# GpSimd normalises every row tile but the last, and four engines get new written-out orders

## The reference

```
mask = adj > 0                                  # adj is 4096 x 4096, about 0.4% of it set
head = mask / max(sqrt(sum(mask, axis=-1)), 1e-12)
inc  = adj + head
y    = x + (inc @ x) / sum(inc, axis=-1)        # x is 4096 x 256
out  = (y - mean(y)) / sqrt(var(y) + 1e-5)      # over the 256 columns of a row
```

## Time and profile before

| | us |
|---|---|
| median of 3 runs | 413.19 |
| lowest and highest run | 411.52, 413.34 |
| profiled execution | 410.89 |
| span of its trace | 409.1 |

### The profile page before, as it was taken

One profiled execution on the slowest core, in us unless ns is written; L12 is line 12 of the kernel. 1 busy time (PEld: TensorE's weight loads), 2 busy tenths in 40 slices (PEclk: granted clock), 3 DMA queues, 4 the chain that ended last, 5 costly groups with the idle time before them and its releaser, 6 DMA issues.

```text
span 409.1 us, 8775 instructions
## 1 busy us (share of the span) xinstructions
PE 389.3 (95%) x2224; PEld 343.1 (84%) x2224; DVE 364.2 (89%) x757; ACT 371.4 (91%) x507; POOL 346.3 (85%) x222
## 2 busy tenths in 40 slices
PE   1689999999999999999999999999999999999995
PEld 0668889988888878888888888888888888888884
DVE  0897999999999999999999999999999999999932
ACT  4967999999999999999999999999999999998530
POOL 3111599999999999999999999999999999999970
PEclk9999999999999999999999999999999999999999
DMA  8999997576677667667666665767666666670020
GB/s 237 269 253 253 264 261 215 168 238 204 200 221 222 190 187 215 190 206 222 200 208 205 195 205 191 208 216 214 197 210 201 196 206 192 215 218 27 27 64 13
DMA packets 36183, 80.00 MB, mean 196 GB/s; under 512 B 9536, under 2 KB 17728, under 8 KB 36160
## 3 DMA queue, kind: packets, MB, share of 16 engines
q1 hardware_dynamic: 35776, 78.68, 66.1%
q10 hardware_dynamic: 384, 1.05, 0.8%
HBM read 75.50 MB, written 4.19 MB: 195 GB/s over the span
## 4 chain that ended last, share of the span: by engine, by line
PE 83%; POOL 4%; issue 4%; SPq 4%; DMA 3%; DVE 1%; ACT 1%; POOLq 0%; ACTq 0%
PE edge L1307 46%; PE edge L1321 23%; PE edge L1258 12%; POOL inc_split L564 3%; DMA x_stage<-in_x_dram 3%; SPq L156 3%; PE sums L1253 1%; SPq L179 1%; DVE incT L767 1%; POOL inc_split L578 0%; PE sums L1232 0%; SPq L184 0%; POOL small L548 0%; DVE inc L751 0%; ACT scaled L251 0%
## 5 line engine op out<-in xcount | busy, mean ns | idle before, releaser
L564 POOL TENSOR_TENSOR inc_split<-incT,inc_split 128x960 fp32r<-128x960 f32 x120 | 269.4, 2272 | 2.4 <-ACT inc_split L262 0.5
L1307 PE MATMUL edge<-x_split,inc_split 128*128 128x512 f32 (+1 forms) x930 | 223.4, 392 | 0.1
L1307 PEld LDWEIGHTS edge<-x_split,inc_split 128*128 128x128 f32 x930 | 168.1, 188 | 32.8 <-ACT inc_split L262 0.9
L751 DVE SCALAR_TENSOR_TENSOR inc<-raw,scaled 128x1024 f32<-128x1024 f32 x128 | 154.3, 1206 | 3.3 <-ACT scaled L251 2.4
L767 DVE STREAM_TRANSPOSE incT<-inc 128x1024 f32<-128x1024 f32 x128 | 156.3, 1230 | 0.7 <-PE edge L1258 0.4
L251 ACT ACTIVATE scaled<-raw,small 128x1024 f32<-128x1024 f32 x128 | 141.1, 1107 | 2.8 <-DVE inc L751 1.2
L240 ACT ACTIVATE sign_out<-raw 128x1024 int8<-128x1024 f32 x128 | 133.7, 1045 | 4.5 <-DMA raw<-in_adj_dram 4.3
L1321 PEld LDWEIGHTS edge<-x_split,inc_split 128*128 128x128 f32 x900 | 112.2, 191 | 2.3
L1321 PE MATMUL edge<-x_split,inc_split 128*128 128x256 f32 x900 | 113.5, 283 | 0.0
L262 ACT CAST inc_split<-incT 128x960 fp32r<-128x960 f32 x90 | 86.5, 984 | 0.7 <-DVE incT L767 0.7
L583 POOL TENSOR_TENSOR small<-small 128x1 f32<-128x1 f32 x24 | 13.2, 554 | 37.2 <-DVE small L733 37.0
(11 more groups left out here) (42 smaller groups left out, 138.8 us busy)
## 6 DMA issues: line engine op xcount, KB each, us to landing
raw<-in_adj_dram SPq DMA_DIRECT2D x504, 128.0 KB, 2.5
rows<-in_x_dram SPq DMA_DIRECT2D x32, 128.0 KB, 2.1
out_dram<-rows SPq DMA_DIRECT2D x32, 128.0 KB, 1.7
x_stage<-in_x_dram SPq DMA_DIRECT2D x12, 256.0 KB, 9.4
raw<-in_adj_dram ACTq DMA_DIRECT2D x8, 128.0 KB, 5.1
x_stage<-in_x_dram SPq DMA_DIRECT2D x4, 192.0 KB, 13.6
x_native<-in_x_dram SPq DMA_DIRECT2D x4, 64.0 KB, 5.7
```

The source lines that it names most:

```text
L564: nc.gpsimd.tensor_tensor(lo_of(s, q), incT[:, s, 0:SPLIT, q, :], hi_of(s, q).bitcast(fp32), ALU.subtract).then_inc(lo_by_pool, 1)
L751: nc.vector.scalar_tensor_tensor(inc[:, q, :], raw[:, s, q, :], 0.0, scaled[q % 2][:, :], ALU.is_gt, ALU.add, accum_out=part_sums[:, s, 0, ...
L1307: last = nc.tensor.matmul(edge[s][:, c0:c1], inc_split[s][:, 0, b, :, :].rearrange("p q j -> p (q j)"), x_split[:, b, :, :].rearrange("p h ...
```

## The change

1. `shift_of`, the `shift` columns and its semaphore are gone. `normalise_by_dve` is gone from DVE, and `normalise` from ACT.
2. POOL gets a `normalise(t, s)` for tiles 0 to 30: one `tensor_scalar`, (y - mean) * rstd, both factors being columns of one element per partition. Tile 31 stays on DVE.
3. In the loop the wait for 1/std stands on the instruction before it (`low_quarter(..., rstd_of_tile=...)`).
4. The orders of ACT, DVE and POOL, and the places of the sums on PE, are new: the written-out part now covers tiles 0 to 17, and the loops start at tile 18. SP's list is not changed.

```diff
 # ACT
-            def normalise(t, s):
-                act.wait_ge(shift_ready, t - 3)
-                nc.scalar.activation(y[:, s, :], y[:, s, :], ACT.Identity, scale=norm_rstd[:, s, G:G + 1],
-                                     bias=shift[:, s:s + 1]).then_inc(result_ready, 1)
 # POOL
+            def normalise(t, s, alone=0, own=True):
+                if alone:
+                    pool.wait_ge(rstd_ready, alone)
+                elif own:
+                    pool.wait_ge(norm_ready, t + 5 - EARLY)
+                nc.gpsimd.tensor_scalar(y[:, s, :], y[:, s, :], mean_var[:, s, 0:1], norm_rstd[:, s, G:G + 1],
+                                        ALU.subtract, ALU.mult).then_inc(result_ready, 1)
-            with pool.Fori(7, PAIRS - 2) as u:
+            with pool.Fori(9, PAIRS - 2) as u:
                 norm_of(2 * u + 1, 1)
                 low_quarter(2 * u, 0, 0, behind=1)
                 round_quarter(2 * u, 0, 1, own=False)
-                low_quarter(2 * u, 0, 1)
+                low_quarter(2 * u, 0, 1, rstd_of_tile=2 * u - 3)
+                normalise(2 * u - 3, 1, own=False)
                 low_quarter(2 * u, 0, 2)
                 low_quarter(2 * u, 0, 3)
...
 # POOL, the end
             low_quarter(31, 1, 1)
+            normalise(28, 0, alone=3)
             low_quarter(31, 1, 2)
             low_quarter(31, 1, 3)
             rstd_of(30, 0)
+            normalise(29, 1, alone=4)
+            normalise(30, 0, alone=5)
             rstd_of(31, 1)
 # ACT's loop, one tile of the two
-                scale_quarter(2 * u, 0, 2)
                 sign_quarter(2 * u + 1, 1, u, 2)
                 sign_quarter(2 * u + 1, 1, u, 3)
+                scale_quarter(2 * u, 0, 2)
                 round_quarter(2 * u, 0, 0)
                 scale_quarter(2 * u, 0, 3)
                 sign_quarter(2 * u + 2, 0, u + 1, 0)
                 scale_quarter(2 * u + 1, 1, 0)
-                sign_quarter(2 * u + 2, 0, u + 1, 1)
                 scale_quarter(2 * u + 1, 1, 1)
-                normalise(2 * u - 3, 1)
                 round_quarter(2 * u, 0, 2)
                 round_quarter(2 * u, 0, 3)
-                scale_quarter(2 * u + 1, 1, 2)
+                sign_quarter(2 * u + 2, 0, u + 1, 1)
                 sign_quarter(2 * u + 2, 0, u + 1, 2)
                 sign_quarter(2 * u + 2, 0, u + 1, 3)
+                scale_quarter(2 * u + 1, 1, 2)
...
 # DVE's loop, one tile of the two, as it is after
+            with dve.Fori(9, PAIRS - 2) as u:
                 inc_quarter(2 * u, 0, 0)
+                inc_quarter(2 * u, 0, 1)
                 degree(2 * u - 2, 0)
+                transpose_quarter(2 * u, 0, 0)
+                transpose_quarter(2 * u, 0, 1)
+                inc_quarter(2 * u, 0, 2)
+                count_of(2 * u + 1, 1)
                 inverse_degree(2 * u - 2, 0)
                 y_first(2 * u - 2, 0, u - 1)
+                transpose_quarter(2 * u, 0, 2)
+                inc_quarter(2 * u, 0, 3)
                 y_second(2 * u - 2, 0)
+                transpose_quarter(2 * u, 0, 3)
                 statistics(2 * u - 2, 0)
                 mean_variance(2 * u - 2, 0)
                 variance_eps(2 * u - 2, 0)
-                shift_of(2 * u - 3, 1)
...
```

More of the change, by code:

```diff
@@ new lines, in _ @@
+            sign_quarter(18, 0, 9, 1)
+            round_quarter(16, 0, 3)
+            scale_quarter(17, 1, 2)
+            sign_quarter(18, 0, 9, 2)
+            sign_quarter(18, 0, 9, 3)
+            scale_quarter(17, 1, 3)
+            sign_quarter(19, 1, 9, 0)
+            round_quarter(17, 1, 0)
+            scale_quarter(18, 0, 0)
+            scale_quarter(18, 0, 1)
+            sign_quarter(19, 1, 9, 1)
+            round_quarter(17, 1, 2)
+            round_quarter(17, 1, 3)
+            with act.Fori(9, PAIRS - 2) as u:
@@ L638, in _ @@
             low_quarter(6, 0, 3)
+            norm_of(8, 0)
             round_quarter(7, 1, 1)
-            norm_of(8, 0)
+            normalise(4, 0)
             low_quarter(7, 1, 0)
@@ L647, in _ @@
             round_quarter(8, 0, 1)
+            normalise(5, 1)
             low_quarter(8, 0, 1)
@@ L652, in _ @@
             round_quarter(9, 1, 1)
+            normalise(6, 0)
             low_quarter(9, 1, 0)
@@ L656, in _ @@
             low_quarter(9, 1, 3)
+            norm_of(11, 1)
             round_quarter(10, 0, 1)
-            norm_of(11, 1)
             low_quarter(10, 0, 0)
+            normalise(7, 1)
             low_quarter(10, 0, 1)
@@ L673, in _ @@
             low_quarter(12, 0, 2)
+            norm_of(14, 0)
             low_quarter(12, 0, 3)
-            norm_of(14, 0)
+            normalise(10, 0)
             round_quarter(13, 1, 1)
@@ L680, in _ @@
             low_quarter(13, 1, 3)
-            with pool.Fori(7, PAIRS - 2) as u:
+            norm_of(15, 1)
+            low_quarter(14, 0, 0)
+            round_quarter(14, 0, 1)
+            normalise(11, 1)
+            low_quarter(14, 0, 1)
+            low_quarter(14, 0, 2)
+            low_quarter(14, 0, 3)
+            norm_of(16, 0)
+            round_quarter(15, 1, 1)
+            low_quarter(15, 1, 0)
+            normalise(12, 0)
+            low_quarter(15, 1, 1)
+            low_quarter(15, 1, 2)
+            low_quarter(15, 1, 3)
+            norm_of(17, 1)
+            low_quarter(16, 0, 0)
+            round_quarter(16, 0, 1)
+            normalise(13, 1)
+            low_quarter(16, 0, 1)
+            low_quarter(16, 0, 2)
+            low_quarter(16, 0, 3)
+            norm_of(18, 0)
+            round_quarter(17, 1, 1)
+            low_quarter(17, 1, 0)
+            normalise(14, 0)
+            low_quarter(17, 1, 1)
+            low_quarter(17, 1, 2)
+            low_quarter(17, 1, 3)
+            with pool.Fori(9, PAIRS - 2) as u:
                 norm_of(2 * u + 1, 1)
@@ L690, in _ @@
                 round_quarter(2 * u + 1, 1, 1, own=False)
-                low_quarter(2 * u + 1, 1, 1)
+                low_quarter(2 * u + 1, 1, 1, rstd_of_tile=2 * u - 2)
+                normalise(2 * u - 2, 0, own=False)
                 low_quarter(2 * u + 1, 1, 2)
@@ L1099, in _ @@
             mean_variance(11, 1)
-            transpose_quarter(13, 1, 3)
             variance_eps(11, 1)
-            with dve.Fori(7, PAIRS - 2) as u:
+            inc_quarter(14, 0, 1)
+            degree(12, 0)
+            inc_quarter(14, 0, 2)
+            inverse_degree(12, 0)
+            y_first(12, 0, 6)
+            y_second(12, 0)
+            transpose_quarter(14, 0, 0)
+            transpose_quarter(14, 0, 1)
+            count_of(15, 1)
+            statistics(12, 0)
+            mean_variance(12, 0)
@@ new lines, in _ @@
+            transpose_quarter(14, 0, 2)
+            inc_quarter(14, 0, 3)
+            variance_eps(12, 0)
+            transpose_quarter(14, 0, 3)
+            degree(13, 1)
+            inc_quarter(15, 1, 0)
+            inc_quarter(15, 1, 1)
+            transpose_quarter(15, 1, 0)
+            transpose_quarter(15, 1, 1)
+            inverse_degree(13, 1)
+            count_of(16, 0)
+            inc_quarter(15, 1, 2)
+            inc_quarter(15, 1, 3)
+            transpose_quarter(15, 1, 2)
@@ new lines, in _ @@
+            y_first(13, 1, 6)
+            y_second(13, 1)
+            transpose_quarter(15, 1, 3)
+            inc_quarter(16, 0, 0)
+            statistics(13, 1)
+            transpose_quarter(16, 0, 0)
+            mean_variance(13, 1)
+            inc_quarter(16, 0, 1)
+            transpose_quarter(16, 0, 1)
+            variance_eps(13, 1)
+            degree(14, 0)
+            inc_quarter(16, 0, 2)
+            count_of(17, 1)
+            inverse_degree(14, 0)
+            y_first(14, 0, 7)
@@ new lines, in _ @@
+            transpose_quarter(16, 0, 2)
+            y_second(14, 0)
+            statistics(14, 0)
+            inc_quarter(16, 0, 3)
+            transpose_quarter(16, 0, 3)
+            inc_quarter(17, 1, 0)
+            mean_variance(14, 0)
+            transpose_quarter(17, 1, 0)
+            inc_quarter(17, 1, 1)
+            variance_eps(14, 0)
+            degree(15, 1)
+            inc_quarter(17, 1, 2)
+            inverse_degree(15, 1)
+            y_first(15, 1, 7)
+            y_second(15, 1)
@@ L1204, in _ @@
-            shift_of(29, 1, alone=4)
             degree(30, 0)
@@ new lines, in _ @@
+            sum_early(3, 2)
+            tile(2, 0, {("hi", 7): lambda: sum_early(3, 3), ("hi", 23): lambda: sum_early(4, 0),
+                        ("lo", 17): lambda: sum_early(4, 1)}, first=True)
+            tile(3, 1, {("native", 0): lambda: [sum_degree(2, 0), sum_early(4, 2)], ("hi", 0): lambda: sum_early(4, 3),
+                        ("hi", 9): lambda: sum_early(5, 0), ("hi", 11): lambda: sum_degree(3, 1),
+                        ("lo", 3): lambda: sum_early(5, 1)})
+            tile(4, 0, {("hi", 0): lambda: sum_early(5, 2), ("hi", 5): lambda: sum_early(5, 3),
```

(1 more changed line is left out.)

523 lines of the change are left out of this document (256 added, 267 removed).

## The result

The kernel after took **433.12 us** (median of 4 runs, 431.79 to 434.47), the kernel before 412.51 beside it: ratio 1.050, 95% interval 1.046 to 1.054. The forecast of 412.9 (411.0 to 416.8) was too low by 20 us.

The account below looks back on a forecast made before the run. PE was taken as the bound at 11.55 us per tile; freed ACT gives -1.9 us, POOL's normalises take back 1.6, so 410.89 - 0.3 = 410.6, plus 2.3 to the median: 412.9 us, range 411.0 to 416.8.

Parts of the forecast that it names:

- the size of n: On POOL, what one new normalise adds from start to next start: taken as 0.45 us, between 0.27 and 0.56.
- outermost bound: Upper limit on n: the full 1.01 us of the one-input rounding over 960 columns.
- The slope: 27 normalises stand ahead of `norm_of(31)` on POOL's unbroken list, so each 0.01 us in n adds 0.27 us at the end.
- the recorded sum: Whole kernel: 410.89 - 0.3 = 410.6 us for an execution like the profiled one, plus 2.3 to the median: 412.9.
- the recorded formula: End of `norm_of(31)` on POOL without waits: 374.9, minus 9.5 of waits, plus 27 x n; 377.5 at n = 0.45.
- GpSimd becomes the bound: Rival: POOL's list sets the pace, gain used up from n = 0.46; 415.9 us at n = 0.56; chance 0.20.
- The value of -1.9 for the freed ACT: Tiles 9 to 14: ACT rid of its normalises no longer delays PE's hi products; -1.9 us, bounds 0 and -1.9.
- the gap moves: Rival: the gap of tiles 9 to 14 moves to another place through the new orders; 414.5 us; chance 0.05.
- The ring through SP: Rival: loads queued behind stores come late, 23.5 us against 2 x 11.55; 2.4 us from tile 18 on, 415.3; chance 0.11.
- The end: Last tile: residual load behind `store(29)`, waiting for POOL's late normalise; value 0 by a hair, bounds 0 and +1.
- The beginning: Up to tile 4: x lands near 28.2 us as before, PE runs without gap; value 0, bounds -0.3 and +0.5.
- The sign of being wrong: Prediction wrong if the beginning up to tile 4 moves over 0.5 us, or PE's steady period leaves 11.55 without POOL or a load before it.

Follow-up runs that it names:

- the first kernel of forms: Whole computation left out; 14 GpSimd instruction forms timed six times each, VectorE idle: at 256 columns, subtract-multiply by two columns 1.20 us, multiply-multiply 0.535.
- the second: Whole computation left out; a second table of GpSimd forms, VectorE idle, asking which pairs are cheap: a single multiply by a constant took 0.81 us.
- n = 0.37 and ACT's stores: Kernel after with GpSimd's normalise as (y * 1.0) * 1.0 and stores of tiles 14 to 26 issued by ACT instead of SP: 413.07 us (1.0015).
- the swap of two entries: Old orders with GpSimd normalising tiles 4 to 30 (453.02 us), now with load_residual ahead of store in SP's list: 433.55 us (1.053).

## Why the prediction was wrong

**The step that failed is the size of n.** "I take n = 0.45, above the middle of 0.27 and 0.56"; measured 1.20 (38.2 us for 31, overlap taken off). It lay above even the "outermost bound" of 1.01. None of the three bounds came from a row with the same pair of operations: 0.27 and 1.01 rest on L578 in the earlier trace rows, a multiply-multiply, and 0.56 is a power, where the normalise is a subtract-multiply. The bound assumed that 256 columns can't cost more than 960; at 3.33 against 0.83 ns per column they can. The one subtraction in the trace, L564's with two inputs (2272 ns for 960 columns), would not have given the price either: with two inputs and 256 columns, GpSimd took 0.68 us start to start for a subtraction (L84 in the first kernel of forms) and 0.68 for a multiplication (L84 in the second), so that row tells nothing of the operation.

**The slope was right.** "Every 0.01 us in n is 0.27 us at the end." With n = 1.20 the recorded sum gives 412.9 + 27 x 0.75 = 433.2, and 433.1 was measured; `norm_of(31)` ends at 398.6, by the recorded formula at 374.9 - 9.5 + 27 x 1.20 = 397.8. That the sum comes within 0.1 is partly luck: PE's last product ended at 426.2, where 404.1 + 20.3 = 424.4, and the sum adds 2.3 from an execution to the median, where the profiled one of after lies 1.35 above its median. The rival "GpSimd becomes the bound" named the mechanism, its place and its threshold; only its price, taken at n = 0.56, was too small. It had a chance of 0.20. POOL's wait for the count went to 0.4 us, as it said.

**The value of -1.9 for the freed ACT failed too.** It is hidden in after, where POOL sets the pace. With n = 0.37 and ACT's stores, where nothing hides it, tiles 9 to 14 still lose 2.2 us against 1.9 before; the rival "the gap moves", with a chance of 0.05, came nearest, except that the gap stayed. Four normalises taken from ACT in the old orders gave 0.4 us in these tiles and about 1.0 in the medians. ACT's normalise stood before the gap in the chain, but so did a late quarter of `adj`, for which ACT waited 0.81 us before and 0.28 + 1.02 us in the kernel with ACT's stores. The bounds of 0 and -1.9 held it for the four; taking the outer one did not. What makes that quarter late was not tested.

**The ring through SP** stood among the rivals with 23.5 us against 2 x 11.55. At n = 1.20 it plays no part, since POOL never waits. At 0.54 it cost 3.3 us and at 0.37 2.0 (3.0 by the ratios), shown by taking the store out of SP's list; the estimate was 2.4 at 0.45.

**The end** was given 0, bounds 0 and +1. The first half of the last tile starts at 426.83 in after, where PE's last product ends at 422.32 + 3.85 = 426.17: DVE waits 4.2 us for x rows there (before, for PE), and the term is +0.7.

**The beginning** was to stay within 0.5 us up to tile 4; it is 80.04 against 78.91. The sign of being wrong that the prediction named thus came. The other kernels with these orders have 78.13 to 80.68 there, those with the old orders 78.65 to 79.46, and each is one execution: PE waits for the first pieces of x, 2.4 us in after and 0.6 before. Whether the orders have a share in it these traces can't tell.

By the rule on the **shared ports** that the prediction cites (the Trainium skill, SBUF — State Buffer), POOL's own instructions could be held up by DVE as well. The last two normalises, with DVE idle, took 2.43 us for two, just as long as amid its work, so no run here shows it for POOL.

On the rates: the Trainium skill, GPSIMD Engine Reference, section 3.1, gives 1.03 cycles per element for up to two operations. The trace agrees for multiply-multiply (0.83 ns, an estimated 1.0 cycle at the page's 1.2 GHz), but not for subtract-multiply, whose 3.33 ns are an estimated 4.0 cycles. Why one pair has the fast rate and the other doesn't, no run here shows.

## What to carry to other kernels

Take the price of a GpSimd instruction only from a row with the same pair of operations; otherwise measure it, or write the formula as one of the fast pairs (here `(y + (-mean)) * rstd` for `(y - mean) * rstd`: 0.54 us for 1.20). Where work goes to the engine with the least room, price it per tile against that engine's waits, since everything beyond them is multiplied by the number of tiles. And treat a DMA queue whose entries wait for a slow engine as part of the loop: a store issued from another queue took 2 to 3 us off, and the swap of two entries 19.5.

None of these kernels is clearly better than before: the best, with four normalises on GpSimd, is 0.25% faster (0.08 to 0.43%).

## What the runs showed of the hardware that was not expected

- GpSimd, `tensor_scalar`, fp32, 128 partitions, per column: 0.83 ns for multiply-multiply, 3.33 for subtract-multiply (3.39 us for 960 columns).
- A single multiplication is slower than a fast pair: 0.81 us by a constant against 0.37, at 256 columns.
- Column operands cost about 0.17 us per instruction, whatever the width (0.33 against 0.17 us at 16 columns).
- VectorE, with GpSimd idle, did the same subtract-multiply of 256 columns in 0.41 us where GpSimd took 1.20.
- A store issued by ACT showed 0.34 to 0.40 us in ACT's queue. The sign it stood beside kept its 1.04 us; the next one started 1.04 to 1.27 us after it, once 1.65, where 1.05 is usual.
